# A transformer layer with cross attention and top-1 experts: bounds, low halves and block keys moved to other engines, and new order tables for the first two chunks

## What is computed

```python
# x (4, 2048, 512), ctx (4, 77, 256), all float32
def xattn(q, kv):                                  # 16 heads of 32 features
    qh, kh, vh = heads(q @ Wq + bq), heads(kv @ Wk + bk), heads(kv @ Wv + bv)
    a = softmax(qh @ kh.T / sqrt(32))              # 2048 x 77 for each head
    return merge(a @ vh) @ Wo + bo
x = x + xattn(layernorm(x), ctx)
n = layernorm(x)
best = argmax(n @ gate_w.T)                        # one of 8 experts
x = x + n + n @ expert_w[best]
```

## Time and profile before

| | |
|---|---|
| median of three runs | 963.38 us (960.46 to 965.33) |
| the profiled execution | 966.26 us, of which the span is 964.4 us |
| busy share of PE / DVE / ACT / POOL | 94% / 80% / 58% / 54% |
| mean granted clock of PE | 0.97 of full speed |

### The profile page before, as it was taken

The page is one execution under the profiler, slowest core; times in us unless marked ns, Lnnn a source line. Parts: engine busy times, 40 slices in busy tenths (PEclk is TensorE's granted clock), DMA queues, the critical chain, the costliest instruction groups (busy, mean ns, idle before and its releaser), DMA issues. The chain is left out here.

```text
span 964.4 us, 27595 instructions
## 1 busy us (share of the span) xinstructions
PE 907.3 (94%) x8840; PEld 544.9 (57%) x8841; DVE 770.7 (80%) x1794; ACT 556.9 (58%) x928; POOL 523.9 (54%) x576
## 2 busy tenths in 40 slices
PE   5999999999899999989999999998897999999995
PEld 3457656566565655656565565665653555555552
DVE  8998889989698988969899898887885555555553
ACT  4686867768486686847768677684842111111110
POOL 2426464664546465454554645546452777777774
PEclk8998999999899999989999999999797999999998
DMA  9323142443414344242433524316544555555550
GB/s 314 103 61 101 51 144 62 138 103 99 146 46 136 88 121 130 68 137 58 136 93 105 142 72 115 96 35 194 212 162 117 167 175 170 164 168 168 173 171 18
DMA packets 81960, 119.52 MB, mean 124 GB/s; under 512 B 20465, under 2 KB 45797, under 8 KB 81839
## 3 DMA queue, kind: packets, MB, share of 16 engines
q1 hardware_dynamic: 69359, 83.74, 32.2%
q0 software_dynamic: 11408, 34.17, 9.4%
q10 hardware_dynamic: 1072, 0.02, 0.1%
HBM read 55.24 MB, written 38.13 MB: 97 GB/s over the span
## 5 line engine op out<-in xcount | busy, mean ns | idle before, releaser
L540 POOL TENSOR_TENSOR p_lo<-pf,p_hi 77x512 f16<-77x512 f32 x128 | 147.1, 1154 | 213.4 <-ACT p_hi L1166 213.1
L1165 ACT ACTIVATE pf<-scoresT,exp_scale 77x512 f32<-77x512 f32 x256 | 174.5, 682 | 74.9 <-PE scoresT L892 60.4
L1664 PE MATMUL mo<-e_w,x2T_hi 128*128 x576 | 184.1, 381 | 0.7 <-DVE x2T_lo L1701 0.7
L1166 ACT ACTIVATE p_hi<-scoresT,exp_scale 77x512 f16<-77x512 f32 x256 | 174.8, 683 | 0.0
L1684 ACT ACTIVATE x2T_hi<-mt 128x512 f16<-128x512 f32 x72 | 43.0, 597 | 179.7 <-PE mt L1653 179.7
L1711 DVE SCALAR_TENSOR_TENSOR res<-mo,inv,row 128x512 f32<-128x512 f32 x72 | 54.1, 751 | 90.7 <-PE mo L1664 90.7
L1253 DVE TENSOR_REDUCE negmax<-work 128x4 f32<-128x308 f32 x256 | 112.6, 468 | 0.3 <-PE work L944 0.3
L1664 PE MATMUL mo<-e_w,x2T_lo 128*128 x288 | 109.8, 381 | 0.0
L1635 POOL DMA_INDIRECT out<-res,row x72 | 71.5, 993 | 64.8 <-DVE xn L1696 56.5
L540 DVE TENSOR_TENSOR p_lo<-pf,p_hi 77x512 f16<-77x512 f32 x128 | 98.4, 784 | 9.4 <-ACT p_hi L1166 7.7
L864 PE MATMUL work<-wo_hi,cT_hi 128*128 128x512 f16 x256 | 97.4, 381 | 0.3 <-DVE cT_lo L1231 0.2
(11 more groups left out here) (262 smaller groups left out, 2171.6 us busy)
## 6 DMA issues: line engine op xcount, KB each, us to landing
row<-rows_by_expert SPq DMA_DIRECT2D x72, 257.5 KB
q_st<-q_hi SPq DMA_DIRECT2D x256, 64.0 KB, 2.0
xt<-in_x SPq DMA_DIRECT2D x15, 1024.0 KB, 8.8
q_st<-q_lo SPq DMA_DIRECT2D x128, 64.0 KB, 2.0
ebuf<-in_L_ffn_expert_w SPq DMA_DIRECT2D x14, 512.0 KB, 7.7
er<-in_L_ffn_expert_w SPq DMA_DIRECT2D x7, 1024.0 KB, 14.7
rows_by_expert<-zrow SPq DMA_DIRECT2D x8, 257.5 KB
out<-res,row POOLq DMA_INDIRECT x72, 2.7
```

Of the source, the lines that this page charges most:

```text
L540: return tt.tensor_tensor(pp[1][0:LK, g % 2, j, :], pf[:, j, :], pp[0][0:LK, g % 2, j, :], ALU.subtract)
L1165: nc.scalar.activation(pf[:, j, :], sbank[n % SB][0:LK, :], ACT.Exp, scale=exp_scale[0:LK, :])
L1166: nc.scalar.activation(pp[0][0:LK, g % 2, j, :], sbank[n % SB][0:LK, :], ACT.Exp, scale=exp_scale[0:LK, :]).then_inc(sem("exp_done"), 1)
L1664: ins = nc.tensor.matmul(obank2[u % 2][:, :], x2T[ia][:, u % 2, k, :], w, start=k == 0 and n == 0, stop=k == KT - 1 and n == 2)
```

## The change

`Wo`'s bound comes from sums of magnitudes, which two ACT instructions take (`OS`) in place of DVE's four maxima; it is a larger bound than the maximum and so gives a coarser scale. The key's low half (`KL`) and those of three of the four query-weight blocks (`WL1` to `WL3`) are subtracted on POOL. For that, ACT also writes the scaled float32 operand back over the raw one. The block keys of all four batches have room (`k_blk`), and one multiplication by a mask, `own_head`, makes them for one batch: batch 0 in the prologue, batches 1 to 3 on POOL in the first chunk of each loop round (`K`). The copy of the next batch's values goes to POOL's queue too (`W`), behind the scatters of the batch's last chunk. DVE no longer clears `k_cur`. SP's first stack of the queries waits for `k_lo` in addition, since the float32 keys lie where it writes. The tables of iterations -1 and 0 are new throughout.

```diff
 GPSIMD = order("""
-    A0 A1 A2 P02 P03 A3 P12 P13 F P22 P23 P32 P33 G D
+    A0 A1 A2 P02 P03 A3 P12 P13 F P22 P23 P32 P33 G D K W
 """)
 GPSIMD_FIRST = order("""
-    LN VO KC F KD
+    VO LN WL1 KC WL2 WL3 KL F
 """)
 GPSIMD_ZERO = order("""
-    P02 P03 P12 P13 P22 F P23 P32 P33 TR A0 A1 A2 A3
+    KD P02 P03 P12 P13 F P22 P23 P32 P33 A0 TR A1 A2 A3
 """)
+        def build_k(tt, b):
+            every = [P, KT, HG, LK]
+            blocks = k_blk[:, bass.ds(b, 1), :, :].rearrange("p a g (j s) -> p (a g) j s", j=HG)
+            tt.tensor_tensor(blocks, k_nat[0][:, :, bass.ds(b, 1), :].to_broadcast(every),
+                             own_head[:].unsqueeze(1).unsqueeze(3).to_broadcast(every), ALU.mult)\
+                .then_inc(sem("k_built"), 1)
@@ stack_queries (SP)
                 if g % 2:
+                    if i.is_(-1):
+                        sp.wait_ge(sem("k_lo"), 1)
                     stack_pair(g // 2)
@@ POOL
+            def key_lo():
+                pool.wait_ge(sem("k_hi"), 1)
+                pool.wait_ge(sem("k_scaled"), 1)
+                nc.gpsimd.tensor_tensor(k_nat[1][:, :, 0:B, :], kf[:], k_nat[0][:, :, 0:B, :], ALU.subtract)\
+                    .then_inc(sem("k_lo"), 1)
+            def query_lo(g):
+                pool.wait_ge(sem("wq_hi"), g + 1)
+                pool.wait_ge(sem("wq_scaled"), g)
+                cols = slice(g * P, (g + 1) * P)
+                nc.gpsimd.tensor_tensor(wq[1][:, :, cols], raw_q[:, :, cols], wq[0][:, :, cols], ALU.subtract)\
+                    .then_inc(sem("wq_lo"), 1)
+                    elif kind == "K":
+                        if not i.static and i.c == 1:
+                            first = Chunk(0, 0)
+                            pool.wait_ge(sem("work_used"), max(use(first, "DK"), use(first, "DB")) + 1)
+                            build_k(nc.gpsimd, i.b + 1)
+                    elif kind == "W":
+                        if i.slot == CPB - 1 and not i.is_(NCHUNK - 1):
+                            wait_alone(pool, "values_ready", 2 * KT * (i.n + 1) + 4)
+                            copy_v(nc.gpsimd, i.plus(1).batch)
@@ ACT
+            def output_sum(k):
+                if k == 0:
+                    act.wait_ge(sem("ld_wo"), 16)
+                part = slice(2 * k, 2 * k + 2)
+                nc.scalar.activation(woT[:, part, :], raw_o[:, part, :], ACT.Abs, accum_out=mo[:, k:k + 1])\
+                    .then_inc(sem("wo_summed"), 1)
@@ DVE
-                    elif kind == "K":
-                        if i.slot == CPB - 1 and not i.is_(NCHUNK - 1):
-                            dve.wait_ge(sem("work_used"), use(i.plus(-1), "M", KT - 1, TPC - 1) + 1)
-                            build_k(nc.vector, i.plus(1).batch)
-                        if (kind, *at) == ("V", KT - 1, 1) and i.slot == CPB - 1 and not i.is_(NCHUNK - 1):
-                            copy_v(i.plus(1).batch)
```

More of the change, by code:

```diff
@@ L297, in build @@
     k_now = sa("k_now", [P, H, LK], F16)
-    k_cur = sa("k_cur", [P, KT, HG * LK], F16)
     v_now = [sa(f"v_now_{s}", [VR, H, VC], F16) for s in ("hi", "lo")]
     v_all = [sa(f"v_all_{s}", [VR, B, H, VC], F16) for s in ("hi", "lo")]
+    own_head = sa("own_head", [P, HG], F16)
     tri = sa("tri", [P, P], BF16)
@@ L328, in build @@
     low = -(-nc.sbuf_base // 64) * 64
-    place = {"q_st": 0, "spare": 16384, "pp": 32768, "pf": 49152, "cc": 57344, "cT": 65536, "nmT": 73728, "xt3": 75776,
-             "experts": 83968, "end": 149504}
+    place = {"q_st": 0, "spare": 16384, "pp": 34816, "pf": 51200, "cc": 59392, "cT": 67584, "nmT": 75776, "xt3": 77824,
+             "experts": 86016, "end": 151552}
     assert low + place["end"] <= nc.sbuf_usable_end
@@ L378, in load_keys @@
                 eng.dma_start(dst[part * DK:(part + 1) * DK, j:H:HG, :], src).then_inc(sem(name), 16)
[L380 to L385, removed]
     def stack_k(tt, b):
@@ L442, in build @@
         blk = st.enter_context(nc.Block())
+        FIRST_BLOCK = KT * HG * LK * 2
+        k_blk = at("k_blk", [P, B, KT, HG * LK], F16, "spare")
+        def build_k(tt, b):
[4 more added lines that the diff above has]
+                .then_inc(sem("k_built"), 1)
         def spare(name, shape, dt, where):
-            return at(name, shape, dt, "spare", where)
+            return at(name, shape, dt, "spare", FIRST_BLOCK + where)
         raw_q = at("raw_q", [P, KT, DM], F32, "cc")
@@ L680, in prologue @@
                 nc.gpsimd.memset(ones[:], 1.0).then_inc(sem("ones_ready"), 1)
+                do(nc.gpsimd.memset(own_head[:], 1.0))
+                do(nc.gpsimd.affine_select(out=own_head[:], in_=own_head[:], compare_op=ALU.is_ge, fill=0.0, base=0,
+                                           pattern=[[-DK, HG]], channel_multiplier=1))
+                do(nc.gpsimd.affine_select(out=own_head[:], in_=own_head[:], compare_op=ALU.is_ge, fill=0.0,
+                                           base=DK - 1, pattern=[[DK, HG]], channel_multiplier=-1))
                 nc.gpsimd.memset(pows[:, 0, :], -0.5)
@@ L725, in iteration @@
                         rank_tables()
+                    elif kind == "KL":
+                        key_lo()
+                    elif kind == "WL":
+                        query_lo(*at)
                     elif kind == "KD":
@@ L943, in banked @@
                         pe.wait_ge(sem("k_built"), i.plus(1).batch + 1)
-                    return nc.tensor.matmul(ps[:, 0:HG * LK], q[0][:, g, t * P:(t + 1) * P], k_cur[:, g, :],
-                                            start=True, stop=True)
+                    keys_of = k_blk[:, bass.ds(i.plus(1).batch, 1), g, :].rearrange("p a n -> p (a n)")
+                    return nc.tensor.matmul(ps[:, 0:HG * LK], q[0][:, g, t * P:(t + 1) * P], keys_of, start=True,
+                                            stop=True)
                 if kind == "E":
@@ L1117, in sum_piece @@
                     .then_inc(sem("e_summed"), 1)
-            first = {"PZ": clear, "CA": context, "KE": keys, "XN": first_rows, "WQ": query_weight, "KH": key_hi, "DV": value_hi, "WO": output_weight, "BV": bias_columns}
+            first = {"PZ": clear, "CA": context, "KE": keys, "XN": first_rows, "WQ": query_weight, "KH": key_hi, "DV": value_hi, "WO": output_weight, "BV": bias_columns,
+                     "OS": output_sum}
             def iteration(i):
@@ L1401, in clear_keys @@
             def clear_keys():
-                nc.vector.memset(k_cur[:], 0.0)
                 for half in k_nat:
```

68 lines of the change are left out of this document (33 added, 35 removed).

## The result

The changed kernel takes **979.47 us** (median of 4, 978.16 to 982.62). The kernel before took 962.68 us beside it (4 runs, 960.46 to 965.33). The ratio is 1.0181, with a 95% interval of 1.0158 to 1.0203: **16.8 us slower**, where 4.4 us less was forecast. The profiled execution took 980.3 us with a span of 978.5; before it was 966.26 with 964.4.

What follows compares the result with a forecast made beforehand. TensorE, busy 907.3 of 964.4 us, was taken as the bound: other engines' work counts only where it waits. Prologue 1.2, chunk 0 2.0 and loop 1.2 sum to 4.4 us: 963.38 to 959.0 us, range 953.5 to 964.5.

Steps and rivals of the forecast that it cites:

- Up to the first query product: Prologue: nothing gained, rather 0.4 us lost; first query product placed at 27.7, before at 27.32.
- From there PE runs through: Prologue: four query products without waits for low halves; last high half at 39.1 instead of 42.00, 2.9 us gained.
- The prologue's net: Prologue up to the first exponential: 1.2 us gained, between ACT's 1.0 and DVE's 1.6; ends 0 and 2.8.
- Chunk 0: Two waits of ACT for scores, 1.50 and 1.54 us, removed by the new table: 2.0 us gained; ends 0 and 3.0.
- The value copies: Loop: copies leave DVE's way to PE's work, 0.4 us a batch, 1.2 for three; on POOL they move only additions.
- The mask product at no cost: Loop, POOL behind four scatters: its first probability half starts 0.9 us late, hidden by 2.4 us of cover before PE.
- One of the signs of being wrong: Loop: a chunk that holds the mask product is over a microsecond longer than its neighbours.
- The rival of the lockout: Loop: DVE's low halves wait for POOL's mask product and value copies, 4.0 us a batch; 971 us, chance 0.08.
- The rival of the larger gain: End of chunk 0: the clock drop over 83 to 91 us goes away, 3.5 us more gained; 955.5 us, chance 0.24.

Runs made afterwards that it cites:

- keys_behind_f: Changed kernel with the mask product moved on POOL behind the second normalisation, past the additions and first low halves: 964.41 us, ratio to before 1.0005.
- scale_b_first: keys_behind_f, with POOL also waiting in the prologue for scale B before the low halves of weight blocks 2, 3 and the keys: 960.38 us.
- copies_on_dve: keys_behind_f with a batch's two value copies back on DVE, without the wait for scale B: 963.30 us, ratio to before 0.9999.
- both: copies_on_dve with POOL's prologue wait for scale B added: 959.85 us, ratio to the kernel before 0.9950.

## Why the prediction was wrong

The range of 953.5 to 964.5 us missed 979.47 by 15 us, on the side that had a chance of 0.07.

- **Up to the first query product, 0 us: right.** It starts at 27.37 (27.7 forecast, 27.32 before).
- **From there PE runs through, last high half at 39.1: wrong.** It came at 43.05. The sum set POOL's blocks against PE's needs and found three microseconds to spare. That was true of the blocks, and the sizes were close: 1.15 to 1.44 us a weight block, 2.25 for the mask product (2.8 at most was forecast), 2.45 for the keys. What it left out is DVE's way to scale B beside the same row, a dozen short instructions that had no term at all. Three of them lasted 4.6 us together, and scale B came at 33.5. With scale B ahead of the row the step is right: 38.27.
- **The prologue's net, 1.2 us gained: wrong by sign**, 2.14 lost. nmT was forecast at 46.5 and is at 45.48 once scale B is free; 0.8 of that 1.0 us is already in the high half (38.27 against 39.1), so the sum behind it was right to 0.2.
- **Chunk 0, 2.0 us: right in the main**, 1.60 and in the last versions 1.63 (39.76 us). The two waits of the earlier trace rows are 0.59 and nothing; two of 0.64 and 0.83 stand elsewhere.
- **The value copies, 1.2 us gained: the size right, the rest missing.** DVE's 0.4 us a batch is there, and POOL's two copies take 1.27 us (1.2 forecast). The sentence that on POOL they "move only additions" failed: 2.5 us lost over three batches.
- **The mask product at no cost, with 2.4 us of cover: the step that failed and decided.** POOL's own low halves came at 142.7, in time for PE at 144.36, so the cover was there. But it is cover for POOL's work. The time went through DVE, whose cover was POOL's 1.95 us of idle time, and the mask product took 2.25: 15.1 us in three chunks, where the sum had nothing. One of the signs of being wrong says just this, a loop chunk with the mask product over a microsecond longer than its neighbours (47.58 against 39.99 and 39.78).
- **The rival of the lockout, 971 us with 0.08: its mechanism and its place right**, its price 4.0 a batch where 7.4, 1.5 and 6.1 came, and its chance far too low. What spoke against it, that the low half "would meet only the mask product's last 0.5 us", took for granted that it waits for what it meets. The Trainium skill, "SBUF — State Buffer", section "Who interferes with whom", has the loser wait for the whole instruction. By that rule the first low half would have ended near 137.3, an estimate: 0.55 us behind the end of the mask product, 136.79. It ended at 144.4, after the whole row: the measurement goes further than the page.
- **The rival of the larger gain, 955.5 us:** the drop of the clock at the end of chunk 0 stayed, 0.57 over 83 to 91 us as in the earlier trace rows. Its sum took 3.5 us where its own bound was 3.4; nothing hangs on that.

The trace of before could have told. The pair's 2.60 us was halved in the prediction to 1.30 each. Taken apart it is 1.99 and 0.68: the first one starts at 136.25, passes the boundary between POOL's second and third addition at 136.4, and ends at 138.2, 0.55 behind the third. The prediction read the mean, 1.30, as a wait for one instruction. Had I read the two apart, the row's new length would have been the question, and the mask product's 2.25 us against the gap of 1.95 the answer.

The second round shows the other side: there ACT brought POOL's high half 0.70 us late, this gap let DVE in after 3.27 us, and the chunk lost 1.5 us only.

## What to carry to other kernels

Before work goes to GpSimd, look on its timeline at what it joins, not at how much it is. A row of GpSimd instructions that read SBUF, without idle time between them, was for VectorE's low halves (tensor_tensor with both inputs in SBUF) one instruction as long as the row, and the idle time in the row is where VectorE gets in. Find such VectorE instructions beside it, and take their longest, not their mean, from the view of single instructions; a pair's mean hides one that was held. Count the short ones too: they waited for one GpSimd instruction each, and a chain of three lost 4 us that way. If the row must grow, put the new piece where a wait already follows, or make GpSimd wait for the short chain first, as scale B here, whose one wait gave 4.0 us (keys_behind_f to scale_b_first) and 3.5 us (copies_on_dve to both).

## What the runs showed of the hardware

- DVE's low half of 77x512 elements (a tensor_tensor with both inputs in SBUF) takes 0.68 us alone. I followed each one of them that took over 0.8 us, in all thirteen traces, against POOL's timeline: 193, of which 192 end 0.55 to 0.56 us behind the end of a row of POOL instructions that read SBUF. For 75 of these the row had only one instruction left; 117 passed at least one boundary, the longest six (8.15 us). The shortest gap that let one in is 0.23 us; the one exception was let in at a boundary, behind the other low half of its pair.
- Other kinds were let in at a boundary. Forty of 1 to 32 columns, of the kinds tensor_scalar (such as scale B's) and scalar_tensor_tensor, met a POOL instruction with another right behind it, and all ended with the one that they met, 0.02 to 0.05 us behind it. Size alone isn't the difference, since a tensor_tensor of 32 columns did pass one, in each of the thirteen traces. From the kernel before, that one (2172 ns, over the boundary at 673.0 us to the row's end at 674.2) and then a scalar_tensor_tensor of as many columns, which was let in at the boundary at 85.55 us:

```profile
L1343 DVE TENSOR_TENSOR oh<-lg,lmax x1: 2172/2172/2172, 672.1 to 672.1; 128x32 bf16<-128x32 f32 x1
```

```profile
L1276 DVE SCALAR_TENSOR_TENSOR gx<-gx,inv,gate_c x1: 1126/1126/1126, 84.5 to 84.5; 128x32 f32<-128x32 f32 x1
```

The kind of instruction fits all of these; no run changed it alone.

- Two groups with only one input in SBUF aren't longer beside POOL's rows: `cT_lo` and `xnT_lo`, whose other input is in PSUM, take 0.69 us at most in 213 cases that started inside a POOL instruction (two of `xnT_lo` took 1.27 us together from 26.00 on, beside the mask product), and `BATCH_NORM_STATS2` 0.70 at most in 730.
- POOL waits for DVE too. In the changed kernel two DVE instructions with both inputs in SBUF follow each other from 58.75 to 60.09 us, and POOL's low half that starts at 59.27 takes 1.85 us instead of 1.15.
- Why a tensor_tensor isn't let in at a boundary can't be seen in a trace, and stays open.
